# Two batches of attention: GpSimd scales the rows, the first weights come later, two step orders changed

## What is computed

```python
xn = (x - mean(x)) / sqrt(var(x) + 1e-5)                 # per row
q, k, v = xn @ dequant(qw_q), xn @ dequant(qw_k), xn @ dequant(qw_v)
q, k = rope(q), rope(k)
attn = softmax(causal(q @ k.T / sqrt(128)))              # four query heads share one k and v
y_attn = (attn @ v) @ dequant(qw_o)                      # dequant: (int - 8) * scale of 128 rows
combine = top2(softmax(xn @ W_router.T))
y_lin = xn @ W_base.T + b_base + ((xn @ A.T) * combine) @ B.T * 2
out = x + y_attn + y_lin
```

## Time and profile before

| | us |
|---|---|
| median of 3 runs (2128.65 to 2131.18) | 2129.5 |
| the profiled execution, its own time | 2131.67 |
| its span, first to last instruction | 2129.9 |

### The profile page before, as it was taken

One profiled execution on the slowest core, in us unless ns is written; L12 is line 12 of the kernel. 1 busy time (PEld: TensorE's weight loads), 2 busy tenths in 40 slices (PEclk: granted clock), 3 DMA queues, 4 the chain that ended last, 5 costly groups with the idle time before them and its releaser, 6 DMA issues.

```text
span 2129.9 us, 31143 instructions
## 1 busy us (share of the span) xinstructions
PE 2105.0 (99%) x11434; PEld 1795.9 (84%) x11436; DVE 1505.2 (71%) x3024; ACT 1016.2 (48%) x2199; POOL 1217.4 (57%) x1117
## 2 busy tenths in 40 slices
PE   8999999999999999999999999999999999999999
PEld 6888888888888888888888888888888888888887
DVE  6767676776767777676776767677676767767676
ACT  3145454544545455454554545454454545445453
POOL 2656565665655565565665656556565655656532
PEclk9999999999999999999999999999999999999999
DMA  6522222231323222221353423123222223212112
GB/s 216 158 42 67 49 68 55 59 70 43 69 53 72 55 54 61 55 70 44 70 145 85 109 55 66 44 60 80 45 67 45 69 55 60 70 44 66 46 40 55
DMA packets 169112, 145.84 MB, mean 68 GB/s; under 512 B 26368, under 2 KB 125440, under 8 KB 168448
## 3 DMA queue, kind: packets, MB, share of 16 engines
q1 hardware_dynamic: 165504, 137.80, 26.9%
q0 software_dynamic: 2112, 4.19, 0.6%
q10 hardware_dynamic: 1344, 1.85, 0.3%
HBM read 133.06 MB, written 10.75 MB: 68 GB/s over the span
## 4 chain that ended last, share of the span: by engine, by line
PE 94%; DVE 5%; issue 0%; DMA 0%; ACT 0%; SPq 0%
PE ring L1067 44%; PE ring L1196 19%; PE O_ps L1067 19%; PE turned L1207 11%; DVE rope L944 1%; DVE rope L943 1%; DVE rope L945 1%; DVE PT_low L876 1%; DVE stats L832 0%; DMA Y<-in_x 0%; PE turned L1177 0%; PE turned L1117 0%; DVE xnT_low L876 0%; DVE probs L863 0%; DVE Y L929 0%
## 5 line engine op out<-in xcount | busy, mean ns | idle before, releaser
L692 ACT ACTIVATE PT_high<-turned 128x512 fp32r<-128x512 f32 (+3 forms) x771 | 370.5, 489 | 585.7 <-PE turned L1207 566.5
L746 ACT ACTIVATE probs<-probs,negmax 128x128 f32<-128x128 f32 (+7 forms) x512 | 397.1, 776 | 262.4 <-DVE negmax L954 250.5
L876 DVE TENSOR_TENSOR PT_low<-turned,PT_high 128x512 fp32r<-128x512 f32 (+3 forms) x771 | 426.6, 555 | 96.0 <-ACT PT_high L692 87.0
L954 DVE CUSTOM_DVE_ANT_0 probs<-ring,mask_row 128x128 f32<-128x128 f32 (+7 forms) x512 | 384.0, 750 | 65.7 <-PE ring L1196 58.9
L1207 PE MATMUL turned<-ident,probs 128*128 128x128 f32 x2304 | 361.2, 273 | 0.9 <-ACT probs L746 0.9
L637 POOL TENSOR_TENSOR rope<-rope 128x512 f32<-128x512 f32 x160 | 206.8, 1293 | 237.9 <-DVE rope L945 236.8
L651 POOL TENSOR_TENSOR ctx_low<-ctx_f,ctx_high 128x512 fp32r<-128x512 f32 x128 | 165.6, 1294 | 280.6 <-ACT ctx_high L692 280.6
L1207 PEld LDWEIGHTS turned<-ident,probs 128*128 128x128 f32 x2304 | 276.9, 140 | 45.9 <-ACT probs L746 1.2
L1067 PE MATMUL ring<-xnT_high,W_high 128*128 128x512 f32 x768 | 302.9, 394 | 0.0
L1067 PE MATMUL ring<-xnT_low,W_high 128*128 128x512 f32 x768 | 299.9, 390 | 0.0
L1067 PE MATMUL ring<-xnT_high,W_low 128*128 128x512 f32 x768 | 299.7, 390 | 0.0
(11 more groups left out here) (110 smaller groups left out, 3618.4 us busy)
## 6 DMA issues: line engine op xcount, KB each, us to landing
R_sb<-row_sums SPq DMA_DIRECT2D x128, 256.0 KB, 4.0
raw<-in_qw_q SPq DMA_DIRECT2D x64, 256.0 KB, 4.5
scl<-in_scales_q SPq DMA_DIRECT2D x64, 256.0 KB, 8.6
raw<-in_qw_o SPq DMA_DIRECT2D x64, 256.0 KB, 4.1
scl<-in_scales_o SPq DMA_DIRECT2D x64, 256.0 KB, 4.4
raw<-in_qw_k SPq DMA_DIRECT2D x16, 256.0 KB, 4.3
scl<-in_scales_k SPq DMA_DIRECT2D x16, 256.0 KB, 5.5
raw<-in_qw_v SPq DMA_DIRECT2D x16, 256.0 KB, 4.5
```

What stands on the lines that cost most here:

```text
L692: return nc.scalar.activation(dst, src, ACT.Copy)
L746: nc.scalar.activation(probs[:, at], probs[:, at], ACT.Exp, bias=negmax[:, i:i + 1], scale=-1.0, accum_out=sums[:, i:i + 1]).then_inc(exp_ ...
L876: nc.vector.tensor_tensor(out=dst, in0=src, in1=high.bitcast(f32), op=ALU.subtract).then_inc(pt_low, 1)
L954: nc.vector.tensor_tensor_reduce(probs[:, prob_at[i]:prob_at[i] + n], score_place(u, h, i), mask_row[:, TOKENS - n:TOKENS], -1.0, -MASKED, ...
```

## The change

- `normalise` moves from VectorE's program to GpSimd's, for both batches. A new semaphore `rstd_ready`, raised by the last instruction of `norm_scale`, tells GpSimd that mean and factor are there; the wait for the buffer's earlier transposition moves along. In the parked batch the eight scalings stand in front of and between the four `base_low`; in batch 0 the first two stand before the bias of parked tile 6 (`FIRST_ROWS`), the others each behind the transposition two tiles before.
- The fourth to sixth weight of the first group are due at 70, 80 and 90 instead of 48, 56 and 64.
- `EARLY` begins with S T instead of T S. In `LATE` the projection F comes before the two scores, one V between these, and at the end one V comes before O instead of after it.

```diff
+FIRST_ROWS = 6
-EARLY = "T S F T S T V S V S T O O V V"
+EARLY = "S T F T S T V S V S T O O V V"
-LATE = "T T T S S F V T V T V T O V T V T S S O V T V V V"
+LATE = "T T T F S V S T V T V T O V T V T S S V O V T V V"
@@ weights_due
-            t = 24.0 + 8.0 * k if u < 0 else ...
+            t = (24.0 + 8.0 * k if k < 3 else 40.0 + 10.0 * k) if u < 0 else ...
@@ gpsimd
+            def normalise(b, t):
+                width = 2 if b == PARKED else 4
+                n = norm_number[b, t - t % width, t - t % width + width]
+                if seen.new(rstd_ready, n):
+                    pool.wait_ge(rstd_ready, n)
+                if nth(b) or t >= 2:
+                    need = turn_number["turn_x", b, t - 2] if t >= 2 else turn_number["turn_x", PARKED, NT - 2 + t]
+                    if seen.new(turned, need):
+                        pool.wait_ge(turned, need)
+                nc.gpsimd.tensor_scalar(xn[:, t % 2, :], row_tile(b, t), mv[:, t, 0:1], rstd[:, t:t + 1],
+                                        ALU.subtract, ALU.mult).then_inc(xn_ready, 1)
-            for k in range(KT):
-                base_low(k)
+            for t in range(NT):
+                normalise(PARKED, t)
+                if t in (3, 4, 5, 7):
+                    base_low((3, 4, 5, 7).index(t))
+                for _, b, t in turned_now[n]:
+                    if b != PARKED and t + 2 < NT:
+                        normalise(b, t + 2)
                 for _, b, t in based[n]:
                     if b == PARKED:
+                        if t == FIRST_ROWS:
+                            normalise(STARTED[1], 0)
+                            normalise(STARTED[1], 1)
                         add_bias(b, t)
@@ vector
-                own(nc.vector.tensor_tensor(out=r, in0=w, in1=r, op=ALU.mult))
+                nc.vector.tensor_tensor(out=r, in0=w, in1=r, op=ALU.mult).then_inc(rstd_ready, 1)
-            def normalise(b, t):
...
-                nc.vector.tensor_scalar(xn[:, t % 2, :], row_tile(b, t), mv[:, t, 0:1], rstd[:, t:t + 1],
-                                        ALU.subtract, ALU.mult).then_inc(xn_ready, 1)
```

More of the change, by code:

```diff
@@ L164, in weights_due @@
         for k, (v, w) in enumerate(weights):
-            t = 24.0 + 8.0 * k if u < 0 else began[u] + WEIGHT_SPAN * PREPARED.index(w) / len(PREPARED)
+            t = (24.0 + 8.0 * k if k < 3 else 40.0 + 10.0 * k) if u < 0 else began[u] + WEIGHT_SPAN * PREPARED.index(w) / len(PREPARED)
             due[sum(x < t + us for x in at[:-1])].append((v, w))
@@ L367, in build_program @@
         xn_ready = sem("xn_ready")
+        rstd_ready = sem("rstd_ready")
         logits_ready = sem("logits_ready")
@@ L401, in score_place, with row_tile @@
             return ring[:, :, :].rearrange("p a b -> p (a b)")[:, at:at + (i + 1) * P]
+        def row_tile(b, t):
+            return Y[:, t, :] if b == PARKED else rows[t // 4][:, t % 4, :]
         def turned_place(step):
@@ L660, in _ @@
             divided, based = behind(STEPS, 1.9, "values"), behind(STEPS, -2.5, "base")
-            added = behind(STEPS, 0.0, "lora_a")
+            added, turned_now = behind(STEPS, 0.0, "lora_a"), behind(STEPS, 0.0, "turn_x")
             for n in range(len(STEPS) + 1):
+                for _, b, t in turned_now[n]:
+                    if b != PARKED and t + 2 < NT:
+                        normalise(b, t + 2)
                 for _, b, t in based[n]:
                     if b == PARKED:
+                        if t == FIRST_ROWS:
+                            normalise(STARTED[1], 0)
+                            normalise(STARTED[1], 1)
                         add_bias(b, t)
@@ L819, in linear_weight_low @@
                 nc.vector.tensor_tensor(out=low, in0=src, in1=high.bitcast(f32), op=ALU.subtract).then_inc(lin_done, 1)
-            def row_tile(b, t):
-                return Y[:, t, :] if b == PARKED else rows[t // 4][:, t % 4, :]
             def row_stats(b, t):
@@ L996, in _ @@
             norm_scale(PARKED, 0, 2)
-            normalise(PARKED, 0)
-            normalise(PARKED, 1)
             row_stats(PARKED, 2)
@@ L1009, in _ @@
                         norm_scale(PARKED, 2, 4)
-                        normalise(PARKED, 2)
-                        normalise(PARKED, 3)
                     elif s == ("turn_x", PARKED, 2):
@@ L1017, in _ @@
                         norm_scale(PARKED, 4, 6)
-                        normalise(PARKED, 4)
-                        normalise(PARKED, 5)
                     elif s == ("turn_x", PARKED, 4):
@@ L1030, in _ @@
                         mask_rows()
-                    elif s[0] == "turn_x" and s[1] != PARKED and s[2] + 2 < NT:
-                        normalise(s[1], s[2] + 2)
                 for _, u, h, i in scored[n]:
@@ L1054, in _ @@
                             norm_rows(STARTED[1], *((0, 4) if of[0] == 3 else (4, 8)))
-                        if u == PARKED and of[0] == 4:
-                            normalise(STARTED[1], 0)
-                            normalise(STARTED[1], 1)
         @block.tensor
```

2 lines of the change are left out of this document (removed).

## The result

The changed kernel takes 2155.43 us (median of 4 runs, 2155.12 to 2155.98) against 2130.34 for the kernel before on the same chip: a ratio of 1.0119, with a 95% interval of 1.0101 to 1.0136. It is 25 us slower, and 29 us above the forecast of 2126.6. In the profiled execution (its run 2155.62) the span is 2153.8 us, 23.9 more than before.

What follows compares the result with a forecast made beforehand. TensorE was taken as the bound (94% of the chain of waits). Gains 0.25 + 0.19 + 0.47 - 0.1 + 1.3 + 0.8 = 2.9 us gave a 2126.6 us median, range 2121.8 to 2131.5.

Steps and rivals of the forecast that it cites:

- Part 1: Parked batch's rows scaled by GpSimd: 0.64 us per scaling, 0.25 us gained, bounds 1.1 lost and 0.5 gained.
- Tiles 0 and 1: Parked batch's first two scalings: some 0.2 us later, hidden behind VectorE's wait for its next input DMA.
- Part 2: Second batch's rows scaled by GpSimd: gains of 0.19 and 0.47 us from freeing VectorE of eight scalings.
- The room of two paces: Second batch: a scaling may start two paces (3.5 us) before its own transposition, so even 1.29 us is hidden.
- VectorE's relief: Second batch: low parts ready sooner without VectorE's scalings, gaining 0.19 us at 67.37 and 0.47 by the first base product.
- The first rival: Start, 20 to 40 us: the slow clock goes away, 3.3 us saved, 2123.3 us; chance 0.14.
- Part 3: First group's later fourth to sixth weights: price 0.1 us at the first scores, bounds 0 and 2; other delays mostly hidden.
- Part 4: The two orders EARLY and LATE: 1.3 us gained in group 0 and 0.8 us from small gaps.
- EARLY's two waits: Group 0, between heads: a scores step fills two waits for ScalarE's exponentials, gaining 2 x 0.64 = 1.3 us.
- LATE's held parts: LATE: high parts held behind an exponential move low parts by 0.7 and 1.1 us; cost nothing, 0.6 us to spare.
- rival 2: LATE's held high parts make the value product wait 0.16 us at each of 48 places: 7.7 us, 2134.3; chance 0.12.
- Small gaps: EARLY and LATE, gaps behind transpositions: -0.01 us per part, 0.8 us in all, bounds +-0.05 per part.

Runs made afterwards that it cites:

- negated: The changed kernel with the mean negated by VectorE, so GpSimd's scaling adds and multiplies instead of subtracting and multiplying; 2129.96 us, ratio 1.0000 to the kernel before.
- twice: The kernel `negated` with each GpSimd scaling issued twice into the same buffer (1.64 us in all); 2145.66 us, ratio 1.0071.
- early: The kernel before with only EARLY changed to its new order, scalings still on VectorE; 2128.84 us, ratio 0.9996.
- best_old_due: `negated` with new EARLY, old LATE, and the first group's fourth to sixth weights due at 48, 56, 64 as before; 2142.19 us, ratio 1.0059.
- best: `negated` with new EARLY, old LATE, and the first group's fourth to sixth weights due at 58, 66, 74; 2132.36 us, ratio 1.0013.
- warm: The changed kernel, slow scaling kept, with more products of zeros in TensorE's gaps in both batches; 2145.53 us, ratio 1.0074.
- final: `negated` with new EARLY, old LATE, and the first group's fourth to sixth weights due at 70, 76, 90; 2127.03 us, ratio 0.9990.

## Why the prediction was wrong

**Part 1, the scaling's size.** This step failed, and with it the result. "The nearest row is its TENSOR_SCALAR with two constants on 128x512, 0.62 us" took an instruction's kind and shape for its cost. That row adds and multiplies; the new instruction subtracts. It takes 2.08 us, and the stated far end of 1.29 was no bound: it belongs to another kind of instruction. The sentence that I'd be wrong at the root if the scaling took over 1.3 us named the right measurement, but no rival had that case. Had the new one been an add, the row would have been near (0.77). The two columns, the only thing about it that I noted as unseen, are 0.15 us of 2.08.

The Trainium skill (GPSIMD Engine Reference, section 4.1) has GpSimd near line rate on one input. The row of 0.62 us agrees; the subtract row of 1.93 us for the same tile does not, and the measurement decides.

**Part 1, the places.** With the scaling at 0.77 us the step's differences stay as small as told, though the gain at tile 4 doesn't come: in `negated` the transposition of tile 2 starts 0.30 later (told 0.15), that of tile 4 0.09 later (told 0.23 earlier). Tiles 0 and 1, "hidden", aren't at 2.08 us: the first product starts 4.1 us late.

**Part 2.** The room of two paces ("so even 1.29 us would be hidden") isn't tested at 1.29 us; at 1.64 us (`twice`) the second batch loses 13.8. The reasoning of two paces holds while GpSimd has nothing else to do. I had checked its queue for the fourth weight, not for the third weight's scaling and split and the biases, about 6 us of other work between 73 and 84 us, nor VectorE's sum that waits for a bias with the low parts behind it. The gain told for VectorE's relief (0.66 us) is there when the scaling is short: from the parked batch's second base product to the first scores `negated` wins 0.9 us against the trace of the kernel before, though only 0.3 against that of `early`. That the later weights are needed for it was right, and its price of "up to 4 us" too small: 9.8 us between `best_old_due` and `best`, although `best` loses 2.6 of its own behind it. TensorE waits 4.8 us in front of tile 4's transposition, where GpSimd stood 5.0 us before the DMA; from there on a tile takes 3.3 us again.

**The clock.** The first rival had it only as a gain. It said that the slow clock follows TensorE's idle time before tile 4, and didn't ask what longer idle times would do. They made at least 10 of the 25 us (`warm`). In this stretch a wait should have been priced both ways, with the clock held and with the clock lost.

**Part 3.** Price told 0.1 us, bounds 0 and 2; measured 1.24, at the fourth scores. Against the first scores q0's second rotary sum came 1.2 us later (told 1.4) and its low part 2.6 (told 3.3). The words "is wanted only behind the projection of q1 and two transpositions, 6 us after 113.58: hidden" looked at who needs the low part. The high part before it stands in ScalarE's strict queue ahead of a copy that TensorE needs.

**Part 4.** EARLY's two waits in group 0: told 1.3, measured 1.2 to 1.4 in `early`. LATE's held parts, told as free with 0.6 us to spare: free in most groups, 0.6 lost in group 0 and 0.6 to 1.0 in group 8, so of rival 2 two places, not 48. Small gaps: told -0.01 us per part; LATE alone -0.03, EARLY alone nothing, both together +0.01. The changed kernel's groups kept before's time within the 0.05 us told, but for groups 1 (+0.11) and 8 (+0.19).

## What to carry to other kernels

A row bounds a new instruction only if engine, shape and arithmetic operation agree; otherwise the forecast needs a rival in which it costs several times as much, and a short run of the instruction's forms settles it before it moves. In a strict queue ask for every step behind the one delayed, not only for the reader of its result. Here TensorE's longer waits were followed by stretches at 1.2 GHz, so that they cost more than their length; a forecast should price such a wait with both clocks.

## What the hardware showed that was not expected

- GpSimd's TENSOR_SCALAR on 128x512 f32: 0.62 us for add-multiply and 1.93 for subtract-multiply with constants; 0.78 and 2.08 with two columns. Its two-operand TENSOR_TENSOR shows no such difference here: 1.29 to 1.30 us for the subtract that makes W_low (L608), for the multiply of the weight's scales (L598) and for the add of the rotary terms (L654).
- Nearly the same gaps went with different clocks. TensorE's wait before tile 4 is 1.82 us in `negated` and in `final`, and the one at 8 to 9 us is longer in `negated` (1.25 against 0.26). Yet in `negated` TensorE is busy 6.55 of 10 us between 20 and 30 us at a granted clock of 1.00; in the kernel before 7.77 at 0.62, in `final`, with the same scaling as `negated`, 7.89 at 0.69. What decides it stays open. The first scores of `before` and `early`, with the same steps up to there, stand 2.3 us apart, as much as the differences that the orders make.
